# The rows of an expert tile turned by a DMA transpose from SyncE instead of by TensorE

## The reference, cut to what matters

```python
weights, indices = jax.lax.top_k(gate_logits, TOP_K)        # 2 of 8
h = jnp.einsum('bsd,edh->ebsh', x, w1) + b1[:, None, None, :]
xh, gh = jnp.split(h, 2, axis=-1)                           # 1024 values, 1024 gates
act = jax.nn.silu(gh) * xh
out_e = jnp.einsum('ebsf,efd->ebsd', act, w2) + b2[:, None, None, :]
return jnp.sum(sel * weights[..., None], axis=2)
```

## Time and profile before

| | us |
|---|---|
| median of 3 runs | 1410.84 (1409.07 to 1411.31) |
| the profiled execution | 1414.7 |
| its span (first to last instruction) | 1412.7 |
| PE busy in the span | 1273.8 (90%) |
| DVE busy | 1141.0 (81%) |
| ACT busy | 797.1 (56%) |
| POOL busy | 782.9 (55%) |

### The profile page before, as it was taken

How to read it: one execution, slowest core, us unless ns; L and a number is a source line. 1 busy time by engine, 2 the same in 40 slices (tenths; PEclk the granted TensorE clock), 3 DMA queues, 4 the chain that set the end, 5 groups by cost and what they waited for, 6 DMA issues and landing times. The chain is left out here.

```text
span 1412.7 us, 40515 instructions
## 1 busy us (share of the span) xinstructions
PE 1273.8 (90%) x13336; PEld 1052.4 (74%) x13337; DVE 1141.0 (81%) x2631; ACT 797.1 (56%) x1862; POOL 782.9 (55%) x743
## 2 busy tenths in 40 slices
PE   4789999999999999899988899999999999999990
PEld 2456666666666676667677899899999999999990
DVE  4789999999999999899977987768576858685666
ACT  5566666667666766676635344444444444444446
POOL 3367677677766787687775433416061707070771
PEclk9799999999999999999967999999999999999996
DMA  6123322334443223321234331312203120301444
GB/s 216 37 73 121 116 96 88 119 119 134 135 135 99 95 66 124 109 86 57 91 114 150 107 122 30 106 50 74 74 30 119 55 95 30 126 28 33 135 138 157
DMA packets 82097, 137.33 MB, mean 97 GB/s; under 512 B 9120, under 2 KB 64928, under 8 KB 81888
## 3 DMA queue, kind: packets, MB, share of 16 engines
q1 hardware_dynamic: 70880, 92.83, 20.5%
q0 software_dynamic: 10848, 42.32, 9.4%
q10 hardware_dynamic: 288, 1.19, 0.2%
HBM read 98.83 MB, written 37.47 MB: 96 GB/s over the span
## 5 line engine op out<-in xcount | busy, mean ns | idle before, releaser
L1098 PE MATMUL pe<-arena 128*128 128x128 f16 x3408 | 219.5, 221 | 19.9 <-issue 19.9
L1098 PEld LDWEIGHTS pe<-arena 128*128 128x128 f16 x3408 | 203.3, 98 | 25.4 <-issue 24.7
L1098 PE MATMUL pa<-arena 128*128 128x128 f16 x3408 | 218.5, 220 | 0.0
L1555 ACT ACTIVATE arena<-pe,arena 128x128 f32<-128x128 f32 x568 | 161.6, 370 | 75.9 <-PE pe L1098 75.4
L1098 PEld LDWEIGHTS pa<-arena 128*128 128x128 f16 x3408 | 201.1, 98 | 0.0
L1123 PE MATMUL py<-arena 128*128 (+1 forms) x1704 | 197.6, 273 | 1.0 <-DVE arena L2345 1.0
L1688 DVE SCALAR_TENSOR_TENSOR arena<-pa,arena 128x511 f32<-128x511 f32 (+2 forms) x240 | 178.7, 745 | 14.3 <-ACT arena L1196 8.2
L1123 PEld LDWEIGHTS py<-arena 128*128 128x128 f16 x1704 | 163.5, 98 | 19.0 <-issue 1.3
L1727 DVE TENSOR_TENSOR_SCAN arena<-arena,pe 128x512 f32<-128x512 f32 x128 | 148.7, 1203 | 3.2 <-issue 1.8
L2539 POOL TENSOR_SCALAR arena<-arena 128x1536 f16<-128x1536 f32 (+2 forms) x35 | 43.7, 1248 | 185.9 <-DVE arena L2345 180.8
L2297 DVE SCALAR_TENSOR_TENSOR pm<-pa,arena 128x128 f32<-128x128 f32 x284 | 80.5, 351 | 77.7 <-ACT arena L1555 73.9
(11 more groups left out here) (308 smaller groups left out, 2584.9 us busy)
## 6 DMA issues: line engine op xcount, KB each, us to landing
arena<-step_rows SPq DMA_DIRECT2D x64, 512.0 KB, 5.7
arena<-in_w_exp POOLq DMA_DIRECT2D x32, 768.0 KB, 4.8
arena<-queue SPq DMA_DIRECT2D x74, 129.5 KB
answer<-arena SPq DMA_DIRECT2D x71, 128.0 KB
arena<-in_x SPq DMA_DIRECT2D x16, 512.0 KB, 6.5
answer<-zeros SPq DMA_DIRECT2D x10, 512.0 KB, 4.8
arena<-h SPq DMA_DIRECT2D x9, 512.0 KB, 6.1
h<-arena SPq DMA_DIRECT2D x8, 512.0 KB, 3.0
```

What stands on the lines that cost most here:

```text
L1098: ins = pe.matmul(bank[:, f * P:(f + 1) * P], w_split[:, p, hl, d * 2 * FF + col:d * 2 * FF + col + P], x[:, r, d, :], start=(n == 0), sto ...
L1555: ins = e.activation(sg[:, half, f, :], GATE[half][:, f * P:(f + 1) * P], ACT.Silu, bias=b1a[:, bass.ds(ex_, 1), ff], scale=1.0 / S1)
```

## The change

PE's `turn`, its PSUM bank and its semaphore go. The split into fp16 halves is done on rows as they lie: ACT writes `rows_hl[:, b, 0]` from `xq`, DVE writes `rows_hl[:, b, 1] = xq - rows_hl[:, b, 0]`. Then SP issues one DMA transpose of the 128x512 fp16 tile `rows_hl[:, b]` into `x_hl[:, b]`, which is four 128x128 blocks (high and low, each in two column blocks), all in SBUF. The split runs two tiles ahead instead of one. SP's list gets one transpose a tile and one more wait before a load, and the answer is written one step later in it.

```diff
+            def turn_rows(i, r):
+                b = r % WB
+                sp.wait_ge(x_done, WB * i + (r + 1))
+                at_least(sp, f_full[3], WB * i + (r - 2))
+                sp.sem_inc(hop, 1)
+                sp.dma_start_transpose(x_hl[:, b].rearrange("p a (d t) -> p (a d) t", t=P),
+                                       rows_hl[:, b].rearrange("p a n -> p (a n)")).then_inc(x_turned[b], 16)
...
+            sp.wait_ge(m_done, NK * MAMBA_UNITS)
+            turn_rows(0, 0)
+            turn_rows(0, 1)
             sp.wait_ge(pad_ready, 1)
...
             with sp.Fori(1, NGRP) as i:
                 for r in range(WB):
-                    swap_rows(i, r)
+                    row_buffer_free(i, r)
+                    load_rows(i + 1, r)
+                    turn_rows(i, r + 2)
+                    answer_out(i, r - 1)
...
-                pe.wait_ge(pt_free, c3.use("o") + 1)
-                turn(0, 0)
                 chunk_d(c3)
...
-            def turn(i, r):
-                b = r % WB
-                pe.wait_ge(xq_in[b], 16 * (i + (r // WB + 1)))
-                at_least(pe, x_done, WB * i + r)
-                pe.sem_inc(hop, 1)
-                for d in range(KD):
-                    ins = pe.transpose(pt[:, d * P:(d + 1) * P], xq[:, b, d * P:(d + 1) * P], ident[:, :])
-                ins.then_inc(f_t_full, 1)
+            def turned_in(i, r):
+                pe.wait_ge(x_turned[r], 16 * i + 16)
+                pe.sem_inc(hop, 1)
...
             def rows_out(i, r):
-                e.wait_ge(f_t_full, WB * i + (r + 1))
-                e.activation(xh[:, r % WB].rearrange("p d t -> p (d t)"), pt[:, 0:KD * P], ACT.Copy).then_inc(xh_ready, 1)
+                b = r % WB
+                e.wait_ge(xq_in[b], 16 * (i + (r // WB + 1)))
+                at_least(e, x_turned[b], 16 * (i + r // WB))
+                e.sem_inc(hop, 1)
+                e.activation(rows_hl[:, b, 0], xq[:, b, 0:D], ACT.Copy).then_inc(xh_ready, 1)
...
             def tile(i, r, ex_):
-                rows_out(i, r + 1)
+                rows_out(i, r + 2)
...
             def rows_low(i, r):
+                b = r % WB
                 dve.wait_ge(xh_ready, WB * i + (r + 1))
-                dve.tensor_tensor(xl[:, r % WB].rearrange("p d t -> p (d t)"), pt[:, 0:KD * P],
-                                  xh[:, r % WB].rearrange("p d t -> p (d t)"), ALU.subtract).then_inc(x_done, 1)
+                dve.tensor_tensor(rows_hl[:, b, 1], xq[:, b, 0:D], rows_hl[:, b, 0], ALU.subtract).then_inc(x_done, 1)
...
             def first_half(i, r, ex_, expert):
-                rows_low(i, r + 1)
+                rows_low(i, r + 2)
```

More of the change, by code:

```diff
@@ L206, in build @@
         sign = sb("sign", [P, NE])
-        ARENA = 50400
+        ARENA = 51600
         arena = sb("arena", [P, ARENA])
@@ L284, in build @@
         b1a, b1v = carve(NE, 2 * NF), carve(NE, NF)
+        rows_hl = carve(WB, 2, D, dt=F16)
         carve = carver()
@@ L299, in build @@
         e_tab, w_eq, w_row, b_row = carve(NJT), carve(WB), carve(WB), carve(WB, D)
-        xh, xl = carve(WB, KD, P, dt=F16), carve(WB, KD, P, dt=F16)
+        carve(5)
+        x_hl = carve(WB, 2, KD * P, dt=F16)
         sg = carve(2, 4, P)
@@ L416, in build @@
         xh_ready, x_done = sem("xh_ready"), sem("x_done")
+        x_turned = [sem(f"x_turned{i}") for i in range(WB)]
         high0 = sem("high0")
@@ L424, in build @@
         xq_in = [sem(f"xq_in{i}") for i in range(WB)]
-        f_t_full, f_t_free = sem("f_t_full"), sem("f_t_free")
         f_full = [sem(f"f_full{i}") for i in range(4)]
@@ L579, in answer_out, with row_buffer_free @@
             def answer_out(i, r):
+                b = r % WB
                 sp.wait_ge(o_ready, WB * i + (r + 2))
                 sp.sem_inc(hop, 1)
-                sp.dma_start(answer[bass.ds((WB * i + r) * P, P), :], yt[:, r]).then_inc(ans_out[r], 16)
-            def swap_rows(i, r):
+                sp.dma_start(answer[bass.ds((WB * i + r) * P, P), :], yt[:, b]).then_inc(ans_out[b], 16)
+            def row_buffer_free(i, r):
                 sp.wait_ge(w_ready, WB * i + (r + 1))
                 sp.wait_ge(x_halved, WB * i + (r + 1))
+                sp.wait_ge(x_done, WB * i + (r + 1))
                 sp.sem_inc(hop, 1)
-                load_rows(i + 1, r)
-                answer_out(i, r)
             sp.wait_ge(cleared, 16 * CLEAR_STEPS)
             for r in range(WB):
-                sp.wait_ge(w_ready, r + 1)
-                sp.wait_ge(x_halved, r + 1)
+                row_buffer_free(0, r)
                 lead_rows(first, WB + r)
-                answer_out(0, r)
+                turn_rows(0, r + 2)
+                if r > 0:
+                    answer_out(0, r - 1)
             sp.wait_ge(rows_done, 1)
@@ L605, in _ @@
                 for r in range(WB):
-                    swap_rows(i, r)
+                    row_buffer_free(i, r)
+                    load_rows(i + 1, r)
+                    turn_rows(i, r + 2)
+                    answer_out(i, r - 1)
             for r in range(NLEFT):
-                swap_rows(NGRP, r)
+                row_buffer_free(NGRP, r)
+                load_rows(NGRP + 1, r)
+                answer_out(NGRP, r - 1)
+            answer_out(NGRP, NLEFT - 1)
             def rows_away(first, end_):
@@ L1049, in epilogue @@
                 pe.wait_ge(m_done, NK * MAMBA_UNITS)
-                pe.wait_ge(x_done, 1)
+                pe.wait_ge(x_turned[0], 16)
                 gate_bank(0, 0, 0, 0)
-                turn(0, 1)
                 ranks(st)
@@ L1067, in experts @@
                 return [v % 8, (v // 8) % 8, (v // 64) % 8], (v // 512) % 2, v // 1024
-            def turn(i, r):
-                b = r % WB
-                pe.wait_ge(xq_in[b], 16 * (i + (r // WB + 1)))
-                at_least(pe, x_done, WB * i + r)
+            def turned_in(i, r):
+                pe.wait_ge(x_turned[r], 16 * i + 16)
                 pe.sem_inc(hop, 1)
-                for d in range(KD):
-                    ins = pe.transpose(pt[:, d * P:(d + 1) * P], xq[:, b, d * P:(d + 1) * P], ident[:, :])
-                ins.then_inc(f_t_full, 1)
             def hidden(i, r, ex_, halves=(0, 1)):
-                turn(i, r + 1)
+                turned_in(i, r)
                 pe.wait_ge(w_have, ex_ + 1)
@@ L1095, in bank_of @@
                     col = first + (4 * half + f) * P
-                    passes = [(hl, x, d) for d in range(KD) for hl, x in ((0, xh), (0, xl), (1, xh))]
+                    passes = [(hl, x, d) for d in range(KD) for hl, x in ((0, 0), (0, 1), (1, 0))]
                     for n, (hl, x, d) in enumerate(passes):
                         ins = pe.matmul(bank[:, f * P:(f + 1) * P], w_split[:, p, hl, d * 2 * FF + col:d * 2 * FF + col + P],
-                                        x[:, r, d, :], start=(n == 0), stop=(n == len(passes) - 1))
+                                        x_hl[:, r, x, d * P:(d + 1) * P], start=(n == 0), stop=(n == len(passes) - 1))
                 return ins
@@ L1139, in _ @@
             schedule(pe, prologue, first, plain, routed, final, epilogue)
-            turn(0, 2)
+            turned_in(0, 1)
             products(0, 1, 0, (0, 1))
@@ L1144, in _ @@
             result(0, 0, 0)
-            turn(1, 0)
+            turned_in(0, 2)
             products(0, 2, 0, (0, 1))
             result(0, 1, 0)
-            turn(1, 1)
+            turned_in(1, 0)
             products(1, 0, 0, (0, 1))
             result(0, 2, 0)
-            turn(1, 2)
+            turned_in(1, 1)
             products(1, 1, 0, (0, 1))
             result(1, 0, 0)
-            turn(2, 0)
+            turned_in(1, 2)
             products(1, 2, 0, (0,))
@@ L1504, in epilogue @@
                 rows_halved(0, 0)
+                rows_out(0, 1)
                 root_x1(st)
@@ L1578, in _ @@
             e.wait_ge(bias_ready, 2)
-            rows_out(0, 1)
+            rows_out(0, 2)
             high_part(0, 0, 0)
@@ L2090, in epilogue @@
                 root_rows(st)
+                rows_low(0, 1)
                 s3_top(st, ch3)
```

## The result

The changed kernel takes 1400.45 us, the median of 4 executions (1397.07 to 1405.77), against 1411.07 (1409.07 to 1412.2) of the kernel before on the same chip. The ratio is 0.9929, with a 95% interval of 0.9906 to 0.9953. That is 10.0 us less (6.6 to 13.3), where -7.3 was forecast. The profiled execution is the slowest of the four: 1405.77 us, with a span of 1403.8.

The account below looks back on a forecast made before the run. The prediction took PE's list to bound the tiles and DVE's list the start; -12.8 - 1.5 - 1.0 + 8 = -7.3 us took the median from 1410.84 to 1403.5 us, range 1398 to 1416.

Parts of the forecast that it names:

- turns: PE's transposes at each tile's head: 0.21 us saved in each of 61 counted tiles, -12.8 us.
- PE's waits for rows: In PE's tiles: 1.0 us of waits and about 0.5 us of sequencer gaps behind them go, -1.5 us.
- turn of tile 0: In the scan's last chunk: PE's 0.61 us wait for rows and 0.45 us turn go, -1.0 us.
- start: Before PE's loop: tile 3's late load holds ACT, then DVE's plan; loop at 819.4 against 811.38, +8 us (+4 to +15).
- the prediction's own test: In the steady tiles: the prediction is wrong if a tile is not 8.07 us from gate to gate.
- Their two operations stay: ACT and DVE in a steady tile: same operations from SBUF, about 0.05 us more on DVE, no cost in total.
- called hidden: At the scan's end: tile 0's transpose starts about 750.5 and has until about 755, so it costs nothing.
- if PE waits for `x_turned`: On PE: a wait for the transposed rows would show the prediction wrong; 13 us were to hide each steady-tile transpose.
- Rival 1: Before the loop: the start costs little, PE's idle time absorbs it; -15.3 to -11 us, 1395.5 to 1400; chance 0.14.
- rival 2: Before the loop: the start eats the gain, +12 to +15 us, sum -3 to 0, 1408 to 1411; chance 0.18.
- Rival 4: On SP and the DMA engines: the transpose itself is dear, from 3.5 us of SP each; 1413 to 1420; chance 0.12.
- The lock: In POOL's splits: DVE operations with two SBUF inputs wait for POOL; 4.2 us in each split, taken as nothing.

Follow-up runs that it names:

- after_pe_turn: Changed kernel with two 128x128 fp32 transposes of the identity, read by nothing, put back on PE at each tile's head: 1412.25 us, ratio 1.0006.
- no_turn_late_answer: Kernel before without PE's two transposes of a turn (experts' results not computed) and with answers one step later on SP: 1399.23 us, ratio 0.9898.
- before_late_answer: Kernel before with only the answer of a tile written one step later on SP, PE's turns kept: 1407.87 us, ratio 0.9971.
- before_aligned: Kernel before with five words left free ahead of xh and xl, so they start on a multiple of 64 bytes: 1408.06 us, ratio 0.9974.
- load3_first: Changed kernel with the load of tile 3's rows issued on SP ahead of tile 1's transpose and the pads: 1396.57 us, ratio 0.9883.

## Why the prediction was right

**The sum, term by term.** By difference of ratios, each within 2 to 4 us by the intervals:

| term | forecast | measured | by |
|---|---|---|---|
| turns | -12.8 | -10.9, -10.3 | after_pe_turn; no_turn_late_answer against before_late_answer |
| PE's waits for rows | -1.5 | -4.1 | before_late_answer |
| turn of tile 0 | -1.0 | not apart | |
| alignment | none | -3.7 | before_aligned |
| start | +8 | +8.7 with tile 0's turn; 6.5 of it the load | the rest of the sum; load3_first |
| sum | -7.3 | -10.0 | |

The start's 8.7 is what remains: -10.0 + 10.9 + 3.7 + 4.1. It holds only if the parts add up. That the turns come out at 10.9 in one kernel and 10.3 in the other speaks for it, and so do the traces: from the result of tile 7 on the changed kernel is 18.2 us faster, and turns, rows and alignment make 18.7 by their runs.

That the sum came out within 2.7 us is in part luck. The turns gave 1.9 us less than forecast, the start with tile 0's turn cost 1.7 more, the waits for rows gave 2.6 more and the alignment 3.7 that nobody had counted: the errors have both signs.

**The turns.** The mechanism held: the time is PE's to give, not the sequencer's. The size, 12.8, lies within the uncertainty of 10.9 and 10.3. The prediction did not see a condition: it counted the late answer on SP nowhere, and without it the turns give 1.7 us.

**The waits for rows.** Read off as 1.0 us of named waits and 0.5 of gaps; removing what made the rows late was worth 4.1. Waits on a sequencer read "issue" and were left out, but the size of each was not traced further.

**The missed term.** The steady tile was to be 8.07 us, and by the prediction's own test 7.98 makes it wrong there: "Their two operations stay" counted the operations and not where their output starts. That is 3.7 us, more than the whole difference of 2.7 between forecast and result.

**The start.** ACT's wait (7.25 us, "some 7"), DVE behind it and the loop 1.7 us behind the plan came as worked out. The plan came at 813.62, where 817 was forecast. The +8 was about right in size, but not in its parts. It was 6 for ACT's wait and 2 for more waits behind POOL's split. Counted from the end of the scan's part, `gated` of tile 1 (776.64) and the plan's last piece each came 6.2 to 6.3 us later than before, so the 2 us did not come: L2236 takes 3.17 us, as L2218 did before. That makes the loop 6.6 us later. The rest of the 8.7, if it is not noise, is not located: the 4.3 us behind the loop's start are this one execution's.

The transpose of tile 0 was called hidden, and was not. It was issued at 748.00, and PE began with its output at 754.33, 6.3 us later, where 3.1 were taken, after a wait of 1.76 us. So by the prediction's own sign "if PE waits for `x_turned`" it was wrong at the start, for tiles 0 and 2, and right in the tiles. What that cost is not measured apart from the rest of the start.

Rival 1 (the start costs little) falls by load3_first; rival 2 (it costs the whole gain) did not come: a transpose held SP 1.22 us and not 1.7 to 3, and the plan came at 813.62, not after 822.

**SP and the transpose.** Forecast were 1.0 us held (0.36 to 2.09) and 3.1 us to landing; measured 1.22 and 2.5. Rival 4 falls: no wait for a transpose after the start. The Trainium skill, "VectorE: DVE Perf Modes", section "The three transpose paths", led to an estimate of 5.2 us at most for the four blocks; the trace has 2.5 as the median (6.9 at most), so by this case the 1309 ns of a block do not add up.

**The lock.** Taken as nothing, and behind the start nothing it was: PE has no wait for DVE in the six later splits. In the first one, ahead of the loop, it has two, of 1.08 and 2.52 us (803.19, 809.85), where before it had none; they lie in time that PE would otherwise have spent waiting for the plan. But the margin is under one such operation a tile.

## What to carry to other kernels

Before costing what an engine is relieved of, follow what stands behind each wait on the queue that feeds it: here a write of results ahead of a load tied PE to DVE's latest delay, and the relief was worth 1.7 us with it and over 10 without. When a wait is moved to an engine with idle time, ask what stands behind it in that list, above all whether something there feeds back to what is waited for; a harmless wait of PE cost 6.5 us on ACT, and closed to a circle it cost 267. And compare the lengths of untouched instructions before and after: buffers that move can change them.

## What the runs showed of the hardware

- 24 matmuls of 128x128 fp16 took 1.34 us with the moving operand starting on a multiple of 64 bytes of the buffer (after, before_aligned), and 1.36 us with it 44 bytes past one (before). Other places were not tried.
- A DMA transpose of 128x512 fp16 from SBUF to SBUF holds SP for 1.22 us and lands in 2.5 us (medians; 6.9 us is the longest landing). The 71 of them go with a rise of all DMA packets from 82097 to 120720, and the loads were hardly later for it: beside the 7.25 us at the start, ACT waited 2 us for them in all (9.2 us in 6 waits).
- A load whose row SP reads from the plan, next behind an answer, came 1.3 to 2.1 us after it in the kernel before, most often 1.28 or 1.69, though the answer's own issue takes 0.35 (an example: 898.67 to 899.95 above). For the loads of the first tiles, which read nothing from the plan, it was 0.57 and 0.58 us.
